# A rank-update recurrence on one core: part of the outer-product sum moves from TensorE to GpSimd

## The reference

```
sa = einsum('bhij,bhj->bhi', S, a_t)
S  = S * exp(w_t)[:, :, None, :] + sa[..., None] * b_t[:, :, None, :] + v_t[..., None] * k_t[:, :, None, :]
o_t = einsum('bhij,bhj->bhi', S, r_t)
```

## Time and profile before

| what | us |
|---|---|
| median of three runs | 4454.21 (4453.38 to 4456.28) |
| the profiled execution: its own time | 4475.04 |
| its span | 4473.3 |
| PE busy / PEld busy | 3935.0 (88%) / 2685.1 (60%) |
| DVE busy | 3218.0 (72%) |
| ACT busy | 2194.9 (49%) |
| POOL busy | 2060.3 (46%) |
| mean granted PE clock | 0.932 |

### The profile page before, as it was taken

The page is one execution under the profiler, slowest core; times in us unless marked ns, Lnnn a source line. Parts: engine busy times, 40 slices in busy tenths (PEclk is TensorE's granted clock), DMA queues, the critical chain, the costliest instruction groups (busy, mean ns, idle before and its releaser), DMA issues. The chain is left out here.

```text
span 4473.3 us, 72079 instructions
## 1 busy us (share of the span) xinstructions
PE 3935.0 (88%) x23448; PEld 2685.1 (60%) x23448; DVE 3218.0 (72%) x8707; ACT 2194.9 (49%) x7361; POOL 2060.3 (46%) x1668
## 2 busy tenths in 40 slices
PE   5999999999996696988849999999999999936598
PEld 2344444444435464666638888888888888835466
DVE  5777777877745111789869999999999999946310
ACT  2666666666665211444404565555655555613211
POOL 2211211211223421111248888888888888725422
PEclk7999999999996798999979999999999999967699
DMA  4322332332346232244342323232322223166232
GB/s 111 82 74 70 100 79 70 87 88 63 79 96 214 74 128 84 104 169 169 150 102 31 42 34 43 34 42 34 41 35 39 37 36 41 15 181 219 80 127 80
DMA packets 479034, 378.41 MB, mean 85 GB/s; under 512 B 298378, under 2 KB 440997, under 8 KB 472544
## 3 DMA queue, kind: packets, MB, share of 16 engines
q1 hardware_dynamic: 466400, 348.90, 32.0%
q0 software_dynamic: 12288, 25.28, 1.7%
HBM read 222.13 MB, written 159.58 MB: 85 GB/s over the span
## 5 line engine op out<-in xcount | busy, mean ns | idle before, releaser
L750 DVE TENSOR_REDUCE at_neg_max<-at_slot 128x1 f32<-128x512 f32 (+3 forms) x1216 | 745.8, 655 | 247.5 <-PE at_slot L542 244.4
L672 ACT ACTIVATE at_prob<-at_slot 128x512 f32<-128x512 f32 (+1 forms) x1216 | 632.4, 579 | 354.3 <-PE at_slot L562 353.4
L2157 PE MATMUL sc_added<-sc_outer,sc_ident 128*128 128x128 f32 x4096 | 585.5, 286 | 78.8 <-POOL sc_outer L1908 58.0
L2157 PEld LDWEIGHTS sc_added<-sc_outer,sc_ident 128*128 128x128 f32 x4096 | 496.4, 191 | 209.3 <-DVE sc_state L2058 115.0
L1921 POOL TENSOR_TENSOR sc_terms<-sc_seen,sc_pack 128x1024 f32<-128x1024 f32 (+2 forms) x288 | 604.7, 2151 | 13.7 <-PE sc_ps_o L2179 13.7
L2179 PE MATMUL sc_ps_o<-sc_terms,sc_ident 128*128 128x256 f32 x2048 | 607.0, 381 | 2.1 <-POOL sc_terms L1921 2.1
L390 POOL TENSOR_SCALAR_AFFINE_SELECT at_prob<-at_prob 128x512 f32<-128x512 f32 x256 | 162.9, 636 | 888.2 <-ACT at_prob L672 888.0
L2081 ACT ACTIVATE sc_seen<-sc_state 128x512 f32<-128x512 f32 x256 | 153.1, 598 | 749.1 <-DVE sc_decayed L2022 740.2
L542 PE MATMUL at_slot<-at_k_stack,at_q_stack 96*128 96x512 bf16 (+3 forms) x1536 | 459.4, 335 | 22.0 <-DMA at_k_stack<-parts 19.5
L1908 POOL TENSOR_TENSOR sc_outer<-sc_pack 128x2048 f32<-128x2048 f32 x128 | 467.3, 3672 | 5.0
L562 PE MATMUL at_slot<-at_q_stack,at_k_stack 99*128 99x512 bf16 (+3 forms) x1536 | 452.7, 331 | 12.2 <-ACT at_prob L672 11.8
(11 more groups left out here) (306 smaller groups left out, 7155.8 us busy)
## 6 DMA issues: line engine op xcount, KB each, us to landing
packed<-pr_pack SPq DMA_DIRECT2D x16, 3072.0 KB, 13.4
sc_pack<-packed SPq DMA_DIRECT2D x512, 96.0 KB, 3.6
parts<-at_parts SPq DMA_DIRECT2D x96, 256.0 KB
f_up_w<-in_ffn_wi SPq DMA_DIRECT2D x16, 1024.0 KB
f_down_w<-in_ffn_wo SPq DMA_DIRECT2D x16, 1024.0 KB
at_q_stack<-parts SPq DMA_DIRECT2D x32, 384.0 KB
at_k_stack<-parts SPq DMA_DIRECT2D x32, 384.0 KB
slots<-at_no_row SPq DMA_DIRECT2D x2, 4128.0 KB
```

The costliest lines, as they stand in the source:

```text
L672: act.activation(prob[:, first:first + n, q1 - tiles * P:q1], ps[:, 0:n * tiles * P].rearrange("p (n k) -> p n k", n=n), ACT.Exp)\
L750: dve.tensor_reduce(neg_max[:, chunk, qt, h:h + n], ps[:, 0:n * tiles * P].rearrange("p (n k) -> p n k", n=n), AX.X, ALU.max, negate=True) ...
L2157: pe.matmul(added[h][:, 0:HALF], ident[:], outer[m % 2][:, 2 * n + s, h * HALF:(h + 1) * HALF], start=(s == 0), stop=False)
```

## The change

After each half of the span's outer products POOL now waits for its own instruction and adds, for pairs 1 and 3 of the half's four, the outer product of the pair's second step onto that of its first, in place. PE then accumulates for these pairs (1, 3, 5 and 7 of a span) only the first of the two tiles. `AHEAD` counts two more POOL steps; the waits of DVE and PE on `pre` are moved so that DVE still waits for the same step, and PE's pairs 0 and 4 wait for the add behind their half.

```
-        AHEAD = 10
+        AHEAD = 12
+        SUMMED = (1, 3)
...
                         pack[m % 4][:, t, FK * D:(FK + 1) * D].unsqueeze(2).broadcast_to(shape), ALU.mult))
+                    own.done()
+                    by_steps = outer[m % 2][:, t, :].rearrange("p (a q s) f -> p a q s f", q=2, s=2)
+                    of_pairs = by_steps[:, :, SUMMED[0]]
+                    own.up(pool.tensor_tensor(of_pairs[:, :, 0, :], of_pairs[:, :, 0, :], of_pairs[:, :, 1, :], ALU.add))
...
-                        dve.wait_ge(pre, 1 + g * AHEAD + AHEAD - 2)
+                        dve.wait_ge(pre, 1 + g * AHEAD + AHEAD - 4)
...
-                    pe.wait_ge(pre, 1 + g * AHEAD + AHEAD - 1 + n // (PAIRS // 2))
+                    pe.wait_ge(pre, 1 + g * AHEAD + AHEAD - 2 + n // (PAIRS // 2) * 2)
...
-                    for s in range(2):
+                    for s in range(1 if n % (PAIRS // 2) in SUMMED else 2):
                         pe.matmul(added[h][:, 0:HALF], ident[:],
                                   outer[m % 2][:, 2 * n + s, h * HALF:(h + 1) * HALF], start=(s == 0), stop=False)
```

## The result

The changed kernel takes 4461.01 us (median of 20 runs, 4457.18 to 4464.88), the kernel before 4454.84 us beside it (20 runs, 4452.73 to 4456.28). The ratio is 1.0015, its 95% interval 1.0008 to 1.0021: 6.2 us slower, of which the interval allows 3.6 to 9.4. Forecast were +5.6 us and 4459.8 us. The profiled execution of the changed kernel has a span of 4463.2 us; the one before had 4473.3, which says again that one profiled execution is not the median. So what follows compares stretches inside the two traces, not the spans.

The account below looks back on a forecast made before the run. The recurrence was taken as a chain through DVE, with PE answering in time. Start 1.35 plus collision 4.3 plus 0 gave +5.6 us, on the median 4454.2 that is 4459.8 us; range 4451 to 4476.

Parts of the forecast that it names:

- PE's relief is worth 0: PE, pairs 1, 3, 5, 7: 0.48 us less work only lengthens the wait for `decayed`, 0.21 to about 0.7 us.
- the hole of 0.14 us: DVE, before the state add: the pair's only hole, the latency of rank, matmul, state.
- the 48.1 us of DVE's waits: DVE's wait for `add_rank` over the 1500 us stretch, set against PE waiting for `decayed` in 458 of 479 pairs.
- PE answers in time: Recurrence: a chain through DVE, with PE keeping up with it.
- The clock: PE: less work could lower the granted clock; taken as 0, 5 us kept for the range; as rival 4465 us, chance 0.04.
- 16 pairs: PE, spans 0 and 1: at half clock each pair's state add about 0.3 us late, 5 us in all.
- The add's duration: POOL's 128 x 512 add: 1.27 us, with ends of 1.06 and 1.59 us.
- The push: POOL: two adds, each with a wait for itself, delay what follows by 2.69 us a span.
- The collision: DVE's `shift_of` in pair 4, held to POOL's L1921 end: 0 and 0.15 us alternately, 29 x 0.15 = 4.3 us.
- the prediction's own table: Longer-hold rival, by add duration: loss 8.9 us from 1.30 us, 4475 us at 1.40, 4498 us at 1.59; chance 0.21.
- The start: First pair: DVE and PE wait for POOL's first outer products, now also for the add, +1.35 us uncovered.

Follow-up runs that it names:

- e1_pe_only: Kernel before, with PE leaving out the second outer product of pairs 1, 3, 5 and 7 and POOL adding nothing; ratio 1.0004, +1.5 us.
- e5_dose: Changed kernel with a small third POOL instruction behind each add; ratio 1.0165 to the kernel before, +71.7 us.
- e6_dose_psum: `e5_dose` with `shift_of` reading the reciprocal from PSUM, plus an added reciprocal and an empty instruction on DVE; ratio 1.0055 to the kernel before, +24.4 us.
- The dose pair: `e5_dose` and `e6_dose_psum`, the same added POOL load without and with `shift_of` reading PSUM; +71.7 and +24.4 us against the kernel before.
- e4_rstd_psum: Changed kernel with one more DVE reciprocal, written into PSUM, and `shift_of` reading that copy; ratio 1.0015 to the kernel before, +3.8 us.
- e8_after_late: Changed kernel with `from_u` and `from_v` moved behind the second `add_terms` of pair 0; ratio 1.0007 to the kernel before, +2.3 us.
- e10_both: `e4_rstd_psum` with PE's pairs 0 and 4 waiting for the outer products alone, pairs 1 and 5 for the adds; ratio 1.0003 to the kernel before, +0.9 us.
- e13_swap: Changed kernel with the PE waits of `e10_both` and, in pair 4, `sum_dots` ahead of `shift_of`; ratio 1.0007 to the kernel before, +2.9 us.
- e12_count: `e10_both` with one real DVE instruction more a span, a third reciprocal in pair 5; ratio 0.9998 to the kernel before.
- e11_both_nop: `e10_both` with one empty DVE instruction more in pair 5 of each span; ratio 1.0016 to the kernel before, +6.6 us.

## Why the prediction was right

*PE's relief is worth 0.* Shown: `e1_pe_only` has the whole relief and no gain beyond its interval, and the wait for `decayed` grew to 0.66 us as forecast (0.7). The step had one flaw. It said that the hole of 0.14 us is the only one in DVE's chain and read the 48.1 us of DVE's waits as small change. They are mostly pair 0's: 0.62 us once a span, made by PE's four instructions for `from_u` and `from_v` between `decayed` and `add_rank`. It changed nothing here, since no outer product stands there, but the sentence that PE answers in time was true of seven pairs in eight. That PE's busy share is no proof shows in the pair of the earlier trace rows: the eight matmuls of L2157 last 275 ns each (median of before) and lie in 1.16 us together.

*The clock.* The prediction's 16 pairs are those of spans 0 and 1, where PE has no `add_terms` yet: in span 1 of before the loads are busy 16.93 of 25 us at a clock of 1.00, of after 15.27, and the clock is 1.00 too. Its half clock is the 0.50 that the trace of before shows over the eight matmuls of the earlier trace rows. What a pair at half clock loses there, 0.3 us by the prediction's estimate, is shown by no run; where the clock did fall, in `e5_dose`, a fall cost 1.25 us. The clock of after stayed at 1.00 in the stretch, and the chain of `e1_pe_only` shows no loss in spans 0 and 1. In `e5_dose`, where relief and a hold of over 1 us came together, it fell 16 times; in `e6_dose_psum`, with the relief and no hold, it did not.

*The add's duration.* 1.27 us from plain two-input rows; measured:

```profile
L1916 POOL TENSOR_TENSOR sc_outer<-sc_outer x128: 1261/1268/1276, 2281.7 to 3871.0; 128x512 f32<-128x512 f32 x128
```

At the rows' slope of 2.11 ns an element the measured add has a constant part of 0.19 us (1.268 less 512 x 2.11 ns).

*The push.* 2.69 us; L1926's ends moved by 2.69 and 2.70 us in the two kinds of span (medians 9.29 to 11.98 and 9.43 to 12.13 us behind pair 0's state add).

*The collision.* 0 and 0.15 us in turn; measured 0.00 to 0.02 and 0.13 (pair 4's interval 3.468 and 3.606 us against 3.460). 29 x 0.15 = 4.3 us was the term; the chain gives 3.9. Held were 25 spans and not 29: the first, span 5, was not, nor were 11, 29 and 41, where a stall of DVE (last section) ahead of pair 4 had already made the chain late. The other kind of span clears by 0.01 us (2.69 against 2.70), which is finer than the forecast of the add could be; by the prediction's own table an add of 1.30 us would have cost 8.9 us. The mechanism was forecast, and that the sum came within 0.6 us of the median is luck in part.

The dose pair and `e4_rstd_psum` show the mechanism: `shift_of` is held to the end of POOL's instruction with both inputs in SBUF and not with one in PSUM (medians 1.175 and 0.158 us in the pair, 0.157 in `e4_rstd_psum`). The prediction took two SBUF inputs for the only case. Rows of the kernel before, behind the last span, show another, with POOL's third L1921 ending at 3908.56 beside the first and POOL at rest beside the second:

```profile
3908.01 0.58 DVE L1992 TENSOR_SCALAR sc_minus_mean<-sc_sums 128x16 f32<-128x16 f32 x1
...
3913.52 0.18 DVE L1992 TENSOR_SCALAR sc_minus_mean<-sc_sums 128x16 f32<-128x16 f32 x1
```

It has one input, in SBUF, ends 0.03 us behind POOL, and does so in every trace here; inside the spans there is no such instruction. `e8_after_late` shows the hold's other face, which the prediction did not draw: a chain that gets shorter runs into it.

*The start.* +1.35; measured +1.32, gone in `e10_both` and `e13_swap`.

*Nothing else.* With neither term `e12_count` stands at 0.9998 of before and `e13_swap` at 1.0007, whose interval still allows 7 us. What remains of the 6.2 us above 5.2 is inside the interval.

## What to carry to other kernels

Ask of work taken off an engine whether it lies between the two points where the bounding chain enters and leaves that engine; here 109 us of PE work in 1500 lay outside and were worth nothing, and four small instructions a span inside were worth 24 us. Before a helper engine gets more work, look not only at how much rest it has but at what the critical engine does in that rest: one instruction of 0.17 us with two SBUF inputs had been living in it. And a loss of microseconds can be repaired or made by an instruction count, so a repair that adds an instruction needs its own control.

## What was not expected of the hardware

DVE has stalls of 0.35 us without a record of their own, at fixed counts of its recorded instructions (of the 95 in a span of the kernel before, 11 are semaphore waits): 384 apart in `e4_rstd_psum`, `e10_both`, `e11_both_nop` and `e6_dose_psum` (96 a span, 15 stalls in each), 2304 = 6 x 384 apart in the kernel before (95 a span). The changed kernel has 95 too and its stalls are in the same pairs of the same spans, so they are no part of the 6.2 us, but for the three spans that they kept from being held. One real instruction more a span made them wander and saved 2.3 us of chain (1604.9 to 1602.6, in different sets). The distances between stalls of one size are multiples of 128 in all these traces, to within two records; what makes them is shown by no run. Counted are stalls that lengthen a pair's interval; one that fell into a hole of DVE's chain would not be seen in this way.
